# Column scores of a 16-batch attention block from two float32r parts, in 49 rows on each half of the TensorE array, and the third group of values one slot later

## What is computed

```python
q, k, v = [jnp.transpose(qkv[:, :, i], (0, 2, 1, 3)) for i in range(3)]
sm = jnp.exp(jnp.minimum(scale_mul, MAX_SCALE_MUL))
q = _l2norm(q) * sm
k = _l2norm(k)
scores = jnp.einsum('bhqd,bhkd->bhqk', q, k)
probs = jax.nn.softmax(scores, axis=-1)
o = jnp.einsum('bhqk,bhkd->bhqd', probs, v)
```

## Time and profile before

| what | us |
|---|---|
| median of 3 runs | 817.16 (814.09 to 817.36) |
| the profiled execution's own time | 816.26 |
| its span | 814.2 |
| mean granted TensorE clock, share of full | 0.978 |
| PE busy, all of the span | 747.3 (92%) |
| ACT busy; DVE busy; POOL busy | 479.3; 480.9; 334.5 |

### The profile page before, as it was taken

The page is one execution under the profiler, slowest core; times in us unless marked ns, Lnnn a source line. Parts: engine busy times, 40 slices in busy tenths (PEclk is TensorE's granted clock), DMA queues, the critical chain, the costliest instruction groups (busy, mean ns, idle before and its releaser), DMA issues.

```text
span 814.2 us, 15335 instructions
## 1 busy us (share of the span) xinstructions
PE 747.3 (92%) x4800; PEld 544.0 (67%) x4800; DVE 480.9 (59%) x1031; ACT 479.3 (59%) x812; POOL 334.5 (41%) x549
## 2 busy tenths in 40 slices
PE   4789999999996789999999999999888999999997
PEld 2578788888863345665566656666556888888885
DVE  2167998998997655555555556655413544344432
ACT  0335555555543477777777777777655555555553
POOL 1034655555554355555555555555631122222100
PEclk9999999999999699999999999999999999999999
DMA  8831342343303665555556666666500000000001
GB/s 243 286 99 29 99 123 82 115 121 85 105 18 64 117 122 112 111 113 112 111 110 110 116 115 112 111 113 118 106 1 1 14 14 26 27 27 27 14 26 39
DMA packets 84457, 71.09 MB, mean 87 GB/s; under 512 B 22270, under 2 KB 83326, under 8 KB 84414
## 3 DMA queue, kind: packets, MB, share of 16 engines
q1 hardware_dynamic: 83086, 70.38, 37.9%
q10 hardware_dynamic: 1328, 0.16, 0.1%
HBM read 52.94 MB, written 17.43 MB: 86 GB/s over the span
## 4 chain that ended last, share of the span: by engine, by line
PE 48%; ACT 8%; issue 5%; DVE 4%; DMA 2%; POOL 1%; SPq 1%; ACTq 0%; POOLq 0%
PE ps L1642 11%; PE ps L1656 11%; PE ps L1532 6%; PE ps L1518 5%; ACT probsT L873 4%; PE ps L1570 3%; PE ps L1470 3%; PE ps L1462 2%; PE ps L1551 2%; ACT w_ada L902 2%; PE ps L1485 1%; ACT projT L894 1%; DVE qk L1131 1%; DMA parts_dram<-w_ada 1%; PE ps L1454 1%
## 5 line engine op out<-in xcount | busy, mean ns | idle before, releaser
L873 ACT ACTIVATE probsT<-ps 128x1024 f32<-128x1024 f32 x128 | 130.8, 1022 | 47.9 <-PE ps L1518 45.9
L1279 DVE TENSOR_TENSOR hidden_low<-hidden,hidden_high 128x512 fp32r<-128x512 f32 x64 | 46.6, 728 | 107.7 <-ACT hidden_high L984 59.7
L1183 DVE TENSOR_REDUCE neg_max<-ps 128x4 bf16<-128x344 f32 x128 | 64.2, 512 | 57.9 <-PE ps L1485 57.0
L1518 PE MATMUL ps<-q_stack,k_stack 97*128 97x256 bf16 x512 | 78.7, 276 | 8.7 <-ACT probsT L873 6.1
L1518 PEld LDWEIGHTS ps<-q_stack,k_stack 97*128 97x128 bf16 x512 | 42.9, 98 | 65.1 <-ACT probsT L873 29.8
L981 ACT ACTIVATE hidden<-ps,b_fc 128x512 f32<-128x512 f32 x64 | 44.1, 689 | 69.7 <-PE ps L1642 69.6
L1532 PE MATMUL ps<-probsT,v_ones 128*32 128x256 f32 x1024 | 69.3, 389 | 9.6 <-ACT probsT L873 9.5
L664 POOL TENSOR_TENSOR scores<-scores,row_max 128x640 f32<-128x640 f32 x32 | 42.1, 1315 | 77.5 <-DVE row_max L1021 77.5
L1462 PE MATMUL ps<-w_qkv,x1T 128*128 128x512 f32 x128 | 65.0, 632 | 2.8 <-DVE rest L1190 2.8
L1380 PE MATMUL ps<-x_res,w_q 128*128 (+1 forms) x256 | 63.7, 394 | 0.0
L806 ACT ACTIVATE weightT<-ps 80x1024 f32<-80x1024 f32 x32 | 32.6, 1019 | 41.8 <-PE ps L1400 41.8
(11 more groups left out here) (177 smaller groups left out, 1805.5 us busy)
## 6 DMA issues: line engine op xcount, KB each, us to landing
parts_dram<-w_ada SPq DMA_DIRECT2D x96, 128.0 KB
q_stack<-parts_dram SPq DMA_DIRECT2D x96, 128.0 KB, 4.0
k_stack<-parts_dram SPq DMA_DIRECT2D x32, 256.0 KB, 6.5
adj<-in_adj SPq DMA_DIRECT2D x16, 440.0 KB, 3.5
xT<-in_xT SPq DMA_DIRECT2D x16, 256.0 KB, 2.6
x_res<-in_x SPq DMA_DIRECT2D x16, 256.0 KB, 3.6
x_in<-in_x SPq DMA_DIRECT2D x16, 256.0 KB, 2.7
k_stack<-parts_dram SPq DMA_DIRECT2D x32, 128.0 KB, 5.2
```

Of the source, the lines that this page charges most:

```text
L873: nc.scalar.activation(probsT[:, s % 4, :], ps[:, COLS:COLS + 2, :].rearrange("p a n -> p (a n)"), ACT.Exp).then_inc(exp_made, 1)
L1183: nc.vector.tensor_reduce(places[:, :, k], ps[:, ROW_BANKS[n % 2], 0:4 * KP].rearrange("p (a g) -> p a g", a=4), AX_X, ALU.max, negate=Tru ...
L1279: nc.vector.tensor_tensor(hidden_parts[1][:, s % H_SLOTS, :], hidden[:, s % RAW, :], hidden_parts[0][:, s % H_SLOTS, :], ALU.subtract).the ...
L1518: mm = nc.tensor.matmul(ps[:, COLS + j, kt * N:(kt + 1) * N], k_stack[:, par, place, kt * P:(kt + 1) * P], q_stack[:, par, place, :], star ...
```

## The change

It does four things.

1. q and k are split into two float32r parts (high and rest) in place of three bfloat16 parts. Three products (`Q_PARTS = (0, 0, 1)`, `K_PARTS = (0, 1, 0)`) and the bound make 49 rows. The two places of a slot stand on different halves of the array: one in rows 0 to 48, the other in rows 64 to 112, and their matmuls alternate.
2. `mid` on ACT and `low_part` on POOL are gone. POOL gets a copy of the high part of q in bfloat16 (`q_short`) for the row scores. `key_sums` now lies in the memory of `x_hat`, with waits in `normalise`, `high` and `blocks_of_pairs` for it.
3. SP puts the high and the low part in one go, reads back twelve stack pieces (before: ten in eight and two), and writes the row of bounds in two DMAs in place of one.
4. `VALUES` is (3, 4, 7, 9): values 2 stand behind column scores 7.

```diff
-NSLOT = 6
+NSLOT = 3
-Q_PARTS = (0, 0, 0, 1, 1, 2)
-K_PARTS = (0, 1, 2, 0, 1, 0)
+HALF = P // 2
+Q_PARTS = (0, 0, 1)
+K_PARTS = (0, 1, 0)
...
-    q_stack = alloc(attention, "q_stack", [KROWS + 1, 2, H, N], BF16)
-    k_stack = alloc(attention, "k_stack", [KROWS + 1, 2, H, N], BF16)
+    q_short = alloc(attention, "q_short", [P, 2, C2 * N], BF16)
+    q_stack = alloc(attention, "q_stack", [HALF + KROWS + 1, 2, HT, N], F32R)
+    k_stack = alloc(attention, "k_stack", [HALF + KROWS + 1, 2, HT, N], F32R)
...
-    VALUES = (3, 4, 6, 9)
+    VALUES = (3, 4, 7, 9)
...
+        def fetch(stack, par, slot, w, part):
+            for c in range(C2):
+                at = HALF * c + slot * SLOT
+                sp.dma_start(stack[at:at + SLOT, par].bitcast(F32), parts_dram[w, :, part, :, c * N:(c + 1) * N].rearrange("h d n -> d h n")
+                             ).then_inc(stack_in, 16)
...
             if b is not None:
-                get_high_and_mid(b, 1 - par)
-                put_part(b, 1 - par, 2, low_made)
+                get_high(b, 1 - par)
                 get_low(b, 1 - par)
                 max_row(b, 1 - par, 0)
             if f is not None:
-                ge(sp, stack_in, f * (10 * 16))
-                put_part(f, par, 0, high_made)
-                put_part(f, par, 1, mid_made)
+                ge(sp, stack_in, f * FETCHED)
+                put_high(f, par)
+                put_low(f, par)
...
         def blocks_of_pairs(f, par):
             pool.wait_ge(high_made, 2 * (f + 1))
+            ge(pool, s_mm, GROUPS * (f - 1))
...
+            nc.gpsimd.tensor_copy(q_short[:, par, :], parts[:, par, 0, 0, :]).then_inc(short_made, 1)
...
-            for j in range(2):
-                place = 2 * s + j
-                for kt in range(T):
-                    mm = nc.tensor.matmul(ps[:, COLS + j, kt * N:(kt + 1) * N], k_stack[:, par, place, kt * P:(kt + 1) * P],
-                                          q_stack[:, par, place, :], start=True, stop=True)
+            for kt in range(T):
+                for j in range(C2):
+                    at = slice(HALF * j, HALF * j + KROWS + 1)
+                    mm = nc.tensor.matmul(ps[:, COLS + j, kt * N:(kt + 1) * N], k_stack[at, par, s, kt * P:(kt + 1) * P],
+                                          q_stack[at, par, s, :], start=True, stop=True)
```

More of the change, by code:

```diff
@@ L144, in build @@
         row_head = alloc(early, "row_head", [P, HT])
[L145 to L148, removed]
+        with ExitStack() as loaded:
+            w_ada = alloc(loaded, "w_ada", [P, C2, 6 * F])
+        part_pairs = alloc(early, "part_pairs", [P, 2 * 2 * 2 * C2 * N], F32R)
+        parts = part_pairs[:].rearrange("p (a w s n) -> p a w s n", a=2, w=2, s=2)
+        ones_r = alloc(early, "ones_r", [P, H * N // P])
         ada_in, = sems(top, "ada_in")
@@ L607, in rows @@
-        def rows(stack, par, at, n):
-            return stack[at * SLOT:(at + n) * SLOT, par].rearrange("p (h c) n -> p h (c n)", c=C2)
-        def whole(w, part, n):
-            return parts_dram[w, :, part:part + n].rearrange("h a d x -> (a d) h x")
-        def get_high_and_mid(n, par):
-            sp.wait_ge(parts_out, 4 * 16 * (n + 1))
-            ge(sp, st_mm, n * 8 - 8)
-            for slot in range(NSLOT - 1):
-                sp.dma_start(rows(q_stack, par, slot, 1), whole(0, Q_PARTS[slot], 1)).then_inc(stack_in, 16)
-            for slot, m in ((0, 2), (3, 2), (5, 1)):
-                sp.dma_start(rows(k_stack, par, slot, m), whole(1, 0, m)).then_inc(stack_in, 16)
+                sp.wait_ge(high_made, 2 * n + w + 1)
@@ L621, in get_low, with get_high @@
+        def get_high(n, par):
+            sp.wait_ge(parts_out, 2 * 16 * (n + 1))
+            ge(sp, st_mm, n * 8 - 8)
+            for slot in range(NSLOT):
+                if Q_PARTS[slot] == 0:
+                    fetch(q_stack, par, slot, 0, 0)
+                if K_PARTS[slot] == 0:
+                    fetch(k_stack, par, slot, 1, 0)
         def get_low(n, par):
             sp.wait_ge(low_out, 2 * 16 * (n + 1))
-            sp.dma_start(rows(q_stack, par, NSLOT - 1, 1), whole(0, 2, 1)).then_inc(stack_in, 16)
@@ L624, in get_low @@
-            sp.dma_start(rows(k_stack, par, 2, 1), whole(1, 2, 1)).then_inc(stack_in, 16)
+            fetch(q_stack, par, Q_PARTS.index(1), 0, 1)
+            fetch(k_stack, par, K_PARTS.index(1), 1, 1)
         def turn(f, b, c, d, par):
@@ L902, in high @@
                 nc.scalar.activation(parts[:, par, w, 0, :], ps[:, QK_BANK + 1 - w, :], ACT.Copy).then_inc(high_made, 1)
-        def mid(f, par):
-            for w in range(2):
-                act.wait_ge(rest_made, 2 * f + w + 1)
-                nc.scalar.activation(parts[:, par, w, 1, :], rest[:, w, :], ACT.Copy).then_inc(mid_made, 1)
         def turn(f, b, c, d, par):
@@ L935, in turn @@
                     high(f, par)
-                if f is not None and s == 7:
-                    mid(f, par)
             if c is not None:
```

99 lines of the change are left out of this document (52 added, 47 removed).

## The result

The change makes the kernel a little faster. Eight runs of it have a median of 811.27 us (810.58 to 813.58), eight of the kernel before 816.57 (814.09 to 817.36). The ratio is 0.9948, with an interval of 0.9935 to 0.9960. That is 5.3 us, where 16 were forecast. The profiled execution's span is 809.4 us in place of 814.2.

What follows compares the result with a forecast made beforehand. PE was taken to set the pace, nearly without gaps. Gains of 11.9 (full turns), 2.0 (last two turns), 0.7 (values 2) and 1.2 (start) sum to 15.8 us, 816.26 to 800.5; forecast 801, range 796 to 822.

Steps and rivals of the forecast that it cites:

- The sign: Whole kernel: the change was forecast faster, at 0.71, against 0.11 for the same and 0.18 for slower.
- what of g reaches the end: Full turns: five column-score groups count (slots 0, 2, 4, 5, 6), 0.85 us a turn, 11.9 us over fourteen turns.
- The column scores, g = 0.17: PE's column scores: a group of four matmuls falls from 0.44 to 0.27 us, gain g = 0.17 (0.15 to 0.19).
- No drain on either side: PE's values on column strips: start right after transposes at 0.121, scores follow after 16 x 0.0625, so no drain.
- The rival of the drain: Array drains before and after every column group, 0.33 us a group, g = -0.16, 828 us; chance 0.10.
- Side by side: Column scores: the two row halves load and stream together, a pair costing 0.121 to 0.147 us.
- the chains that the forecast had found: Slots 1 to 3: scores 2 and `norm_transposed` wait on other engines, so savings at scores 1 and 3 give nothing.
- The last two turns: Last two turns: PE waits for exponentials between column scores, so six groups in each count, 2.0 us.
- Values 2: Values 2 behind scores 7: worth nothing in a full turn, 0.7 us in the last turn.
- the wait of values 3: Full turn, PE waiting for exponential 7: to become 0.8 us in place of 0.62.
- Parts, copies: ACT and POOL: dropping `mid` and `low_part` gives nothing; the `q_short` copy, about 0.61 us, is hidden with slack 1.1.
- Start: First column scores: the row of bounds comes sooner from SP, saving 1.2 of the 1.43 us wait.

Runs made afterwards that it cites:

- e4: Changed kernel with column-score matmuls reading only the upper 16 bits of each float32r number as bfloat16, on the same halves: 805.82 us, ratio 0.9865.
- e9: Changed kernel with exponential 7 ahead of the second half of `high` on ACT, and values 2 directly behind column scores 7: 805.64 us, ratio 0.9855.
- e5: Changed kernel with both places of a slot read from the lower half (rows 0 to 48), so nothing runs side by side: 839.21 us, ratio 1.0264.
- e1: Kernel before with only values 2 moved behind column scores 7: 815.50 us, ratio 0.9986.
- e2: Changed kernel with values 2 put back ahead of column scores 7: 812.99 us, ratio 0.9960 to the kernel before.
- e8: Kernel before with the second `high` copy behind exponential 7 and DVE's second `rests` in slot 8: 814.84 us, ratio 0.9981.
- e3: Changed kernel with both places' rows stacked without a gap and every column-score matmul over all 98 rows, on the whole array: 824.31 us, ratio 1.0089.
- e10: Changed kernel with values 0 and 1 ahead of the output's transposes, so two more changes of mode in a turn: 823.16 us, ratio 1.0074.

## Why the prediction was off

The sign and the range held; the size did not. Forecast: 16 us from 817.16. Measured: 5.3. The sign held in part by luck, as the point on what of g reaches the end shows.

- **The column scores, g = 0.17: the step that failed.** I costed a pair at 0.121 to 0.147 and a group at 0.27. The group still costs 0.435, and 0.09 more where whole-array work stands ahead, so g was 0.01 to -0.08. Two assumptions fell. "No drain on either side" was read from pitches that had the drain averaged into them. And the loads were costed as in a stream, while the first pair of a group is loaded only after the change of mode. e4 gives 0.10 for the loads. The seam in the records gives 0.10 for the way out, and e9 shows that it is there for strips as well. The third piece is the way in, 0.09. In the kernel before only the slots behind values paid for one. A small piece is that float32r was taken to stream like bfloat16, from durations of 395 and 383; by its starts it takes 0.117 for 256 columns, and bfloat16 0.109.
- The rival of the drain named the right mechanism and both its places. I gave it 0.10 and priced it at 0.33 a group; the two seams measure 0.19, and the exposed loads that it left out another 0.10. With 0.19 alone, g is -0.02 and the same sum comes out near no change. The Trainium skill (TensorEngine Tiling, Key Properties) says that changing the tiling mode drains TensorE. I had written that the trace does not agree for column strips. It does: 0.10 in the kernel before, ahead of the values.
- **Side by side: right.** Starts in pairs, 3 to 4 ns apart, as the Trainium skill (TensorE: Matmul & The Clock Gate, Part 3) has it, and e5 puts the price of not doing so at 0.23 a group.
- **What of g reaches the end.** By the rule of the forecast (five groups of a turn count) a g at or under zero would have given nothing or a loss. The 0.22 a turn came from two things that it did not have. `max_transposed` behind the scores of slots 0 and 5 had been a seam already (row below). It started 0.54 behind scores that begin at 338.36, where row scores start 0.44 behind, and it starts 0.43 behind them now: 0.11 twice. And the last result of a group comes 0.50 after its start, not 0.61, so exponential 6 starts 0.10 sooner behind its scores. Against this stands the way in, 0.09 at scores 6; at scores 1 and 3 it is hidden by the chains that the forecast had found. Followed through the turns that start at 338.36 before and at 335.68 after, the lead over the old turn is 0.14 at scores 6, and 0.24 at exponential 6 and at the end. On the mean it is 0.22, and 13 x 0.22 = 2.9 us.
- **The last two turns** were to give 2.0 and, in the trace, lost 0.5. The forecast took no account of the granted clock there. It was 0.92 in the last turn but one, before and after, and in the last one up to values 3 at 0.83 after the change against 0.91 before. That the change brings this about isn't shown: e1, with the old groups, has 0.75 there.

The timeline of PE in the kernel before, ahead of slot 0's other work:

```profile
338.90 0.28 PE L1491 MATMUL ps<-ident_b,neg_max 128*8 128x128 bf16 x2
```

- **Values 2:** forecast nothing in a full turn and 0.7 at the end. Right in a full turn; at the end open (e1, e2). But the wait of values 3 was to grow to 0.8, and it is 0.32 in the profile's count, or 0.47 as the forecast counted it, from the pitch of the last row scores. With g gone and a seam ahead of the values, PE is done later than I reckoned, and exponential 6 starts 0.10 sooner.
- **Parts, copies:** the copy takes 0.61 as taken from the earlier trace rows, and no row scores wait for it.

POOL's timeline in the kernel after:

```profile
355.28 0.61 POOL L737 CAST q_short<-part_pairs 128x512 bf16<-128x512 f32 x1
...
356.67 2.63 POOL L743 TENSOR_TENSOR key_blocks<-x_hat,row_head 128x688 bf16<-128x688 f32 x2
```

- **Start:** forecast 1.2, with the first scores at 273. They start with no wait for a DMA:

```profile
271.55 0.80 PE L1526 MATMUL ps<-q_stack,k_stack 49*128 49x256 f32 x4
...
273.18 0.38 PE L1499 MATMUL ps<-ident_b,neg_max 128*8 128x128 bf16 x2 [0.83 <-DVE neg_max L1187]
```

The wait of 1.43 is gone, but PE now waits 0.83 for the row maxima on DVE one step later, which the forecast did not look for. The distance from the last row scores ahead of the first column scores to `make_qk(0)` behind them tells the worth without what lies earlier. It is 3.46 us in the kernel before, 3.03 in e1 and 3.02 in e8, and 2.77 in the changed kernel and in e2, e3, e4, e5 and e10. So the start gave 0.25 to 0.7, not 1.2. In this execution the next turn starts 2.2 us sooner than in that of before, but 1.3 of it are there ahead of those row scores already, and that stretch varies: in the nine other kernels with the same start the first scores lie between 271.4 and 274.4.

Of the 5.3 us, then, 2.9 lie in the full turns and 0.25 to 0.7 at the start. The rest is not assigned: it may be the values, or the ends of the attention, which vary between executions.

## What to carry to other kernels

Cost a group of matmuls from start to next start, and cut the averages at the seams: the last start of one kind against the first of the next, never the first start against the next kind's first. Splitting the array's rows makes pairs run together, but a short group between whole-array work pays about 0.1 us on each side and exposes its first loads (another 0.1 us with float32), so it wants long groups, or neighbours in the same mode. And when a wait is left, ask which of two lists (PE's order or ACT's) is late next, since a move in one may be worth nothing without the move in the other.

## What the runs showed of the hardware

- A change of mode costs some 0.10 us with no stream: 0.09 from the whole array into the halves (0.52 against 0.43), 0.10 from halves or whole array into strips, 0.10 from the halves back to the whole array. From halves to strips directly it is paid once (e9). Transposes that fill only 8 columns of the array (`max_transposed`) paid it too: 0.54 behind a group of the kernel before, where row scores came at 0.44.
- No load was pulled ahead over such a change. The first float32 load of 128 columns is exposed for 0.11; with bfloat16 the second pair starts at 0.13 in place of 0.22. In e3_whole a wait for an exponential exposed it in the same way, without a change of mode (0.58 for the group, against 0.48 where PE came straight from whole-array work).
- Loads of the two row halves run side by side: they start 3 to 4 ns apart, as the matmuls do. On one set of rows (e3, e5) the float32r matmuls of 256 columns start 0.12 apart, the bfloat16 ones of the kernel before 0.11.
- Bfloat16 weights read with a stride, as the upper halves of 32-bit words, load at the bfloat16 rate: a record of 96 ns in e4, of 98 ns in the kernel before, of 189 ns with float32.
